# TensorE's step in another order: rounded-type matmuls first, each weighing followed by one head's projection

## The reference

```python
h = jnp.maximum(_layernorm(x, axis=-1), 0.0)
q = (h @ Wq + bq).reshape(b, m, H, d)          # k and v alike
scores = jnp.einsum('bmhd,bnhd->bhmn', q, k) / sqrt(d)
scores = scores + edge_bias[edges].transpose(0, 3, 1, 2)
scores = jax.nn.leaky_relu(scores, 0.2)
scores = where(edges > 0, scores, -1e9)
attn = softmax(scores, axis=-1)
out = jnp.einsum('bhmn,bnhd->bmhd', attn, v).reshape(b, m, H * d)
x = x + out @ Wp + bp
```

## Time and profile before

| | us |
|---|---|
| median of 3 runs (1076.60 to 1079.05) | 1077.94 |
| the profiled execution, own time | 1076.71 |
| its span, first to last instruction | 1074.9 |
| PE busy in the span | 987.5 (92%) |
| PEld busy | 973.3 (91%) |
| DVE busy | 913.9 (85%) |
| ACT busy | 777.3 (72%) |
| POOL busy | 492.5 (46%) |

### The profile page before, as it was taken

The page is one execution under the profiler, slowest core; times in us unless marked ns, Lnnn a source line. Parts: engine busy times, 40 slices in busy tenths (PEclk is TensorE's granted clock), DMA queues, the critical chain, the costliest instruction groups (busy, mean ns, idle before and its releaser), DMA issues.

```text
span 1074.9 us, 32436 instructions
## 1 busy us (share of the span) xinstructions
PE 987.5 (92%) x9055; PEld 973.3 (91%) x9055; DVE 913.9 (85%) x3374; ACT 777.3 (72%) x1721; POOL 492.5 (46%) x865
## 2 busy tenths in 40 slices
PE   2247999999999999999999999999999999999996
PEld 2236999999999999999999989999999999999995
DVE  3625889989999889989999879989999899999984
ACT  1335878777778768777777867777877777778762
POOL 1000445445555545545555544545555455545454
PEclk9985899999999999999999999999999999999998
DMA  8093444433444343433434343434434344434220
GB/s 166 1 290 102 120 138 119 122 107 113 135 114 132 102 131 110 127 110 110 138 111 132 105 132 97 131 104 123 141 99 135 107 135 119 124 112 121 65 80 9
DMA packets 193427, 125.53 MB, mean 117 GB/s; under 512 B 34452, under 2 KB 181908, under 8 KB 193236
## 3 DMA queue, kind: packets, MB, share of 16 engines
q1 hardware_dynamic: 190736, 122.73, 40.0%
q10 hardware_dynamic: 2500, 0.55, 0.4%
HBM read 79.19 MB, written 44.04 MB: 115 GB/s over the span
## 4 chain that ended last, share of the span: by engine, by line
PE 66%; DVE 20%; issue 6%; ACT 2%; DVEq 1%; DMA 1%; ACTq 1%; SPq 1%; POOL 1%; POOLq 0%
PE bank L1197 14%; PE bank L1228 8%; PE bank L1150 7%; PE bank L1287 6%; PE bank L1185 6%; PE bank L1139 5%; PE bank L1140 5%; DVE w L1650 4%; PE bank L1162 4%; PE bank L1174 4%; PE bank L1205 4%; DVE q_lo L1624 3%; DVE onehot L1662 3%; DVE o_all L1749 2%; DVE w L1673 2%
## 5 line engine op out<-in xcount | busy, mean ns | idle before, releaser
L1007 POOL TENSOR_SCALAR a_line<-w,a_bias 128x256 f32<-128x256 f32 x512 | 260.3, 508 | 463.4 <-DVE w L1673 411.2
L1197 PE MATMUL bank<-pt,nat_sb 128*65 128x128 f32 x2048 | 267.2, 274 | 0.1
L1650 DVE CUSTOM_DVE_ANT_0 w<-bank,mask_rows 128x256 f32<-128x256 f32 x512 | 195.7, 419 | 51.8 <-PE bank L1140 36.5
L1426 ACT ACTIVATE pt<-bank 128x512 f32<-128x512 f32 x256 | 153.7, 600 | 116.4 <-PE bank L1150 111.8
L1673 DVE SCALAR_TENSOR_TENSOR w<-w,shift,a_line 128x256 f32<-128x256 f32 x512 | 231.2, 491 | 7.2 <-issue 4.7
L1197 PEld LDWEIGHTS bank<-pt,nat_sb 128*65 128x65 f32 x2048 | 232.3, 139 | 0.6 <-issue 0.6
L1662 DVE TENSOR_TENSOR onehot<-val,counts_to 128x512 fp32r<-128x512 f32 x256 | 177.1, 692 | 9.8 <-DVE val_max L1617 9.2
L1408 ACT ACTIVATE mask_own<-bank,mask_bias 128x512 bf16<-128x512 f32 x256 | 174.5, 682 | 2.4 <-PE bank L1174 2.4
L1150 PE MATMUL bank<-ident,w 128*128 128x128 f32 x1024 | 154.2, 273 | 0.0
L1417 ACT ACTIVATE t_sb<-bank 128x512 fp32r<-128x512 f32 x256 | 149.8, 585 | 5.0 <-PE bank L1162 4.9
L1139 PE MATMUL bank<-t_sb,q_hi 128*128 128x256 f32 x512 | 143.9, 303 | 4.4 <-issue 4.3
(11 more groups left out here) (132 smaller groups left out, 1623.2 us busy)
## 6 DMA issues: line engine op xcount, KB each, us to landing
adj_in<-in_adj_dram SPq DMA_DIRECT2D x64, 512.0 KB, 4.0
mask_store<-mask_own SPq DMA_DIRECT2D x64, 512.0 KB, 3.2
mask_rows<-mask_store SPq DMA_DIRECT2D x512, 64.0 KB, 2.4
stack_store<-stage SPq DMA_DIRECT2D x14, 256.0 KB, 3.1
h_stack<-stack_store SPq DMA_DIRECT2D x7, 512.0 KB, 5.1
h_nl<-nl_store SPq DMA_DIRECT2D x28, 128.0 KB, 3.4
x_res<-in_x_dram SPq DMA_DIRECT2D x16, 128.0 KB, 2.2
nl_store<-nl_rest SPq DMA_DIRECT2D x1, 2048.0 KB, 8.8
```

The source lines that it names most:

```text
L1007: nc.gpsimd.tensor_scalar(a_line[:, i % 2, :], w[:, i, :], 5.0, a_bias[:, i:i + 1], ALU.mult, ALU.add)\
L1197: last = pe.matmul(o_part[0:D + 1, P * u:P * u + P], nat_sb[:, t % 2, p % 4 * 2 + u, k, :], pt[:, p % 2, u, k, :], start=(k == 0), stop=(k ...
L1650: nc.vector.tensor_tensor_reduce(w[:, i, :], row_bank[:, SLOTS * u:SLOTS * u + SLOTS], mask_rows[:, t % 2, p % 4 * 2 + u, :], 0.25, LEAST_ ...
```

## The change

Five things change, in one edit.

1. TensorE's step: all rounded-type matmuls come first (`scores`, `gather_keys`, `gather_masks`, `natural`, `beta`, `q_piece`, the sums), then `turn_y`, then `weigh`, then the bf16 ones (`turn_adj`, `count`, `rank`).
2. `weigh` and `project` are interleaved: behind each of `weigh`'s four matmuls stands the projection of one head.
3. The projection's halves are two steps apart (lags 28 and 30, so steps 0 and 2) instead of one (27 and 28). `NORM` follows (29 and 31), `SUM` goes from 30 to 32, `OUT` from 31 to 33. `COUNT` goes from 6 to 7 and `USED` from 7 to 8; `RANK` stays at 8 but stands at the step's end.
4. ScalarE's `exp`, `copy_o` and `copy_adj` go to the end of its step.
5. VectorE takes counts, flags and ranks (and the first part of `pick_beta`) ahead of `take_scores`; the second part, `keep_beta`, stays where it was.

```diff
-    LOAD, CONV, TURN_A, COUNT, USED, RANK, VAL, ONEHOT = 0, 4, 5, 6, 7, 8, 9, 9
+    LOAD, CONV, TURN_A, COUNT, USED, RANK, VAL, ONEHOT = 0, 4, 5, 7, 8, 8, 9, 9
-    SCORE, A_LINE, Y, TURN, PV, X_ADD, PROJ, NORM, SUM, OUT = 17, 19, 20, 21, 22, 24, 27, 28, 30, 31
+    SCORE, A_LINE, Y, TURN, PV, X_ADD, PROJ, NORM, SUM, OUT = 17, 19, 20, 21, 22, 24, 28, 29, 32, 33
...
-            def weigh(b, p):
+            def weigh(b, p, due, s):
                 n, t = PPG * b + p, p // 4
                 pe.wait_ge(probs_ready, n + 1)
                 pe.wait_ge(nat_copied, n + 1)
                 if later(n):
                     pe.wait_ge(o_copied, n)
+                if due is not None:
+                    free(adj_bank_uses, b, s, len(list(adj_bank_uses(b, s))) - 1)
                 for u in range(2):
                     for k in range(2):
                         last = pe.matmul(o_part[0:D + 1, P * u:P * u + P], nat_sb[:, t % 2, p % 4 * 2 + u, k, :],
                                          pt[:, p % 2, u, k, :], start=(k == 0), stop=(k == 1))
-                last.then_inc(pv_done, 1)
+                        if (u, k) == (1, 1):
+                            last.then_inc(pv_done, 1)
+                        if due is not None:
+                            project(b, *due, 2 * u + k)
...
             def step(b, s):
                 p = pair(b, s, SCORE)
                 if p is not None:
                     scores(b, p)
-                p = pair(b, s, TURN)
-                if p is not None:
-                    turn_y(b, p)
-                p = pair(b, s, PV)
-                if p is not None:
-                    weigh(b, p)
                 due = piece(b, s, TFILL, 4)
...
+                p = pair(b, s, TURN)
+                if p is not None:
+                    turn_y(b, p)
+                p, due = pair(b, s, PV), piece(b, s, PROJ, 2, 2)
+                if p is not None:
+                    weigh(b, p, due, s)
+                elif due is not None:
+                    wait_projection(b, *due, s)
+                    for h in range(4):
+                        project(b, *due, h)
+                t = tile(b, s, TURN_A)
+                if t is not None:
+                    turn_adj(b, t, s)
...
```

More of the change, by code:

```diff
@@ L1215, in count, with rank, wait_projection, project @@
                 last.then_inc(cnt_done, 1)
-            def rank(b, t, s):
+            def rank(b, t, s, i):
                 pe.wait_ge(used_ready, TPG * b + t + 1)
-                free(q_bank_uses, b, s, 0)
+                free(q_bank_uses, b, s, i)
                 pe.matmul(q_bank[:, 0:TPG * GPT], lower[:, :], used[:, t % 2, :], start=True, stop=True)\
                     .then_inc(rank_done, 1)
-            def project(b, t, e, s):
-                n = TPG * b + t
-                pe.wait_ge(o_copied, 4 * n + 4)
+            def wait_projection(b, t, e, s):
+                pe.wait_ge(o_copied, 4 * (TPG * b + t) + 4)
                 free(adj_bank_uses, b, s, len(list(adj_bank_uses(b, s))) - 1)
[L1227 to L1230, removed]
+            def project(b, t, e, h):
+                last = pe.matmul(adj_bank[:, (D + 1) * h:(D + 1) * h + D + 1], ot_sb[0:D + 1, t % 2, 4 * e + h, :],
+                                 w_ext[0:D + 1, 4 * e + h, :], start=True, stop=True)
+                if h == 3:
+                    last.then_inc(proj_done, 1)
             def step(b, s):
@@ L1250, in step @@
                     natural(b, p)
[L1251 to L1259, removed]
                 i = 0
[L1261 to L1264, removed]
                 due = beta_piece(b, s, BETA)
@@ L1303, in step @@
                     pe.matmul(misc[:, 0:D], mean_rep[:, :], w_sum[:, :], start=True, stop=True).then_inc(vec_done, 1)
+                p = pair(b, s, TURN)
[9 more added lines that the diff above has]
+                t = tile(b, s, TURN_A)
+                if t is not None:
+                    turn_adj(b, t, s)
+                t = tile(b, s, COUNT)
+                if t is not None:
+                    count(b, t, s)
+                t = tile(b, s, RANK)
+                if t is not None:
+                    rank(b, t, s, i)
                 if isinstance(b, int) and b == B - 1 and s == K0 + 16:
-                    free(q_bank_uses, b, s, i)
+                    free(q_bank_uses, b, s, i + 1)
                     pe.wait_ge(flag_steps, 9)
@@ L1487, in step @@
                     nc.scalar.activation(vecs[:, bass.ds(D * (b + g), D)], misc[:, 0:D], ACT.Copy).then_inc(vec_ready, 1)
+                p = pair(b, s, TURN)
+                if p is not None:
+                    exp(b, p)
+                p = pair(b, s, PV)
+                if p is not None:
+                    copy_o(b, p)
+                t = tile(b, s, TURN_A)
+                if t is not None:
+                    copy_adj(b, t)
             for s in range(K0):
@@ L1677, in step @@
                     take_counts(b, t)
+                t = tile(b, s, USED)
+                if t is not None:
+                    flag_used(b, t)
+                t = tile(b, s, VAL)
+                if t is not None:
+                    take_ranks(b, t)
+                due = beta_piece(b, s, BETA + 1)
+                if due is not None:
+                    pick_beta(b, *due)
                 p = pair(b, s, SCORE)
```

27 lines of the change are left out of this document (8 added, 19 removed).

## The result

The changed kernel takes 1124.15 us (1119.12 to 1128.68, 4 runs) against 1077.27 us for the kernel before (four runs; the 1077.94 ahead of the prediction was the median of three): ratio 1.0432, 95% interval [1.0382, 1.0482]. It is 4.3% slower; 1048 us was forecast, 1038 to 1066 the range, and slower had a chance of 0.09. The profiled execution has a span of 1120.6 us and a granted clock of 0.959, 0.974 before.

A forecast was written before the change was run, and what follows sets the result against it. PE was taken as the bound, DVE 5% behind. Interleaving -0.30, neighbours +0.05, hole -0.27 make -0.52 us a tile, -31 over 60 tiles; with 3 lost to coupling, 1076.7 becomes 1048.7, predicted as 1048, range 1038 to 1066.

The forecast's parts named there:

- Pass prices and the interleaving: On PE, alternating weighing and projection passes cuts two of each from 0.442 to 0.391 us: -0.30 us a tile.
- rival of a broken overlap: Alternating shapes on PE stop loads overlapping streams: 0.164 us a head, 84 us, 1132 us in all; chance 0.09.
- margin of 0.4 us: In step 1, the slack for the ranks' bank to be freed before the queries' piece needs it: 0.4 us.
- the hole moves elsewhere: Rival: PE waits for the ranks' bank before step 1's queries' piece; 1064 us; chance 0.10, shared with load not short.
- sign of being wrong: In the profile after, PE waiting at the queries' piece for `val`, among other places, by over 0.1 us a tile.
- POOL: cost 0: POOL's step 0, about 4.9 us of work, costs 0, up to 0.3 us a tile if DVE stretches the adds.
- The prediction's chain for this step: DVE's step 0: 0.65 + 0.7 (scores) + 0.8 (q_lo) + 0.7 (one-hot), ending 2.9 us in.
- The hole at `turn_adj`: PE's wait there for VectorE's `norm` (`o_all`) goes, as `turn_adj` stands last in step 1: -0.27 us a tile.
- The 0.5 us of cover: In step 1, `norm` ends at 2.7 us and `turn_adj` starts at 3.2, so the wait is covered by 0.5 us.
- DVE becomes the bound: Rival: DVE loses as many waits as before, a graph takes 116.5 to 117 us: 1059 us; chance 0.17.
- The chances: Whole kernel: faster 0.88, same 0.03, slower 0.09; the forecast itself (1042 to 1054) 0.60.
- The range's best end: PE's full -31 us and the hole at 0.30 us: given as 1040 us, rather lower.

The follow-up runs named there:

- e8: e2 with POOL's three additions over heads cut to one column each (heads not summed): 1052.94 us, ratio 0.975.
- e12: e8 with the projection's four heads in one block behind the weighing, not interleaved: 1062.41 us, ratio 0.985.
- e2: The changed kernel with only beta and the two sums moved to the end of TensorE's step: 1079.81 us, ratio 1.001.
- e13: The changed kernel, sums in front, with POOL's three additions cut to one column (heads not summed): 1090.57 us, ratio 1.011.
- e9: The kernel before with POOL's three additions cut to one column (heads not summed): 1072.03 us, ratio 0.994.
- e3: The changed kernel with the projection's four heads in one block behind the weighing, not interleaved: 1126.98 us, ratio 1.046.
- e1: The changed kernel with beta, queries' pieces, sums and ranks all behind the turns, weighing and bf16 matmuls: 1086.68 us, ratio 1.008.
- e7: e2 with VectorE taking the ranks first in its step 1: 1066.52 us, ratio 0.988.
- e5: The kernel before with only the changed lags, old order, nothing interleaved: 1115.86 us, ratio 1.033.

## Why the prediction was wrong

**Pass prices and the interleaving: right.** 0.39 us a head in the trace, the short load behind a projection included; 0.30 us a tile between e8 and e12; 115.20 us a graph in e8 where 114.8 was the sum. The rival of a broken overlap is out, and with it the reading that the change is slow because of what it interleaves. The drain that the page "TensorEngine Tiling (Array Packing)" of the Trainium skill (Key Properties) ties to a change of tiling mode does not show between 128x65 and 65x128 operands (0.39 us a head). That fits the page's bound of 64 (Overview, "The Problem"), under which neither shape falls. No matmul of the loop has a stationary operand of 64 rows or columns or fewer, so the drain itself no run here shows.

**The first step that failed: not every moved instruction was followed to its wait.** The prediction has no term for beta and the sums at all, and never asks who frees the bank for them. They are four a graph, stand in even steps, and were moved forward past the point at which `low_q` frees `q_bank`: behind natural without a wait they would start 0.37 us after it, in e2 they start behind the weighing, 2.4 us after it. e2 shows 44 us. The prediction looked at that bank only for the ranks, and there gave a margin of 0.4 us; its rival in which "the hole moves elsewhere" and its sign of being wrong named this wait, at 0.1 us a tile and more. It came at 0.4, but the rival's price, 1064, held nothing of the rest.

**The second: "POOL: cost 0".** I asked when POOL's results are needed, and allowed only that VectorE stretches the additions, not that they stretch VectorE. With `norm`'s halves and `add_heads` shifted, the additions lie in the VectorE step that holds the counts, the flags and two `q_lo`, and right before the ranks for which PE waits. The chain from scores to ranks in step 0 takes 514.98 - 510.79 (the first taking of scores) = 4.2 us, where its parts at their own length come to about 3.3. The prediction's chain for this step also left out the counts and flags in front of the scores: the first taking starts 0.87 us into PE's step and the one-hot ends 3.67 into it, where it had 0.65 and 2.9. That turned the 0.4 us margin into a wait of 0.44 us in this step 1, 0.4 in the mean of a graph. e13 shows 34 us for the additions in the changed kernel, e9 7 us for them in the kernel before. The hint was in front of me: shift at 290 ns in the mean for four columns, 111 more than its twin `shift_neg` (71 of them are the additions' doing, as e9's 219 ns show). In step 2 of the kernel before, beside the additions at 512.09, it starts at 513.48 and takes 0.43 us, against 0.15 in step 0.

The Trainium skill has it: its page "SBUF — State Buffer", section "SBUF: two separate sides", says that VectorE with two SBUF inputs and a GpSimd operation that reads SBUF exclude each other, whoever starts first holding the ports to its end. The 0.72 us of `shift_neg`, to the end of the addition beside it, agree, and so does `q_lo`, which reads PSUM for one input and stays at 477 ns in both kernels.

**The third goes with these: the clock.** The prediction has no term for it. The granted clock between 200 and 1000 us is 0.97 in the changed kernel and in e13 and 0.98 in e3, the three with the sums in front. It is 0.99 in e2 and e8, with the sums at the end, and 1.00 in the kernel before. How much of the 47 us is clock no experiment isolates. The third graph takes 135.10 us against 123.7 before, the fourth 124.10 against 119.0, the fifth 131.7 against 124.0. So the third lost 6 us and the fifth 3 us more than the fourth did, whose clock stayed at 1.00. An estimate of the most that it can be: 0.03 of 800 us, 24 us. What came back with the sums in e2 holds part of it.

**The hole at `turn_adj`: half right.** In the changed kernel it is gone, because the wait in front of the queries' piece covers it. Where that wait was removed it came back (7.2 us a graph in e1, 3.5 in e7), and only without the additions was it 0.3. The 0.5 us of cover were not there: `norm` was to end 2.7 us into PE's step 1, and ends at 516.68, 3.28 us into it.

**The rival "DVE becomes the bound"** had the right engine with the wrong price. VectorE did not lose waits by coupling; its own operations were stretched by 4 us a graph (109.24 to 113.22 busy), and PE asked for their results earlier.

**The chances.** Of a moved block with two shared banks and four engines, 0.88 for faster was too sure: margins of 0.4 and 0.5 us, worked out from one execution, were taken as nothing to pay. The range's best end has a slip too, without effect on the outcome: 1076.7 - 31 - 60 x 0.03 is 1044, not 1040.

## What to carry to other kernels

When a step is written in another order, follow each instruction that moves forward to the wait that stands before it, the rare ones too: here four of them a graph cost 44 us, and the interleaving of the projection's halves brought some 10. Ask of each engine not only when it is done, but what it runs beside; in these traces a small VectorE operation with two SBUF inputs could last as long as what was left of the GpSimd addition that it met. A gain that one engine makes shows only once its waits are gone (2.8 us, within the spread, between e3 and the changed kernel, 9.5 between e12 and e8).

## What was not expected of the hardware

- A four-column VectorE operation beside a GpSimd addition of 128x256 takes 0.72 us, alone 0.16; `used<-cnt`, with a single input, takes 0.74 in the mean where the conversion runs beside it (e5), without it 0.21. Why an operation with a single input is stretched no run here isolates.
- A wait before small sums can come ahead of a fall of the granted clock, but doesn't decide it. PE waited 0.92 us at 226.47, then made sums of two columns, and the clock's mean from 226 to 231 us is 0.66; the weighing's passes there took 0.21 us in place of 0.11, the lower of the two levels. In the fourth and the sixth graph the same four waits, of 0.9 to 1.3 us, left it at 1.00. The changed kernel from 226 to 231 us:

```profile
226.00:231.00 5.00, 4.53 (x28) 4.53 (x28) 2.15 (x8) 1.69 (x4) 0.97 (x2) 0.66 0.56 136
```
